# Attention stage: the input loads, the small transfers of the softmax sums and the shift row issued in another order on SyncE's queue

## The chip, the cores and the metric

The kernel runs on one core of a Trainium2 chip. Its time is the device time of one execution in microseconds, as a median of runs. Five engines work side by side, each through its own instruction stream: PE (TensorE, with its weight loads shown as PEld), DVE (VectorE), ACT (ScalarE), POOL (GpSimd) and SP (SyncE, which here only issues transfers). They wait for each other and for transfers by semaphores.

## The reference

```python
def reference(x, qkv_w, qkv_b, proj_w, proj_b, Wr, br, W1, b1, W2, b2):   # x: 4 x 2048 x 512, fp32
    xn = layernorm(x)
    # attention, 16 heads of 32
    qkv = einsum('bnc,dc->bnd', xn, qkv_w) + qkv_b
    q, k, v = split into heads
    attn = softmax(einsum('bhqd,bhkd->bhqk', q, k) * 32 ** -0.5)
    out = einsum('bhqk,bhkd->bhqd', attn, v)
    a = einsum('bnc,dc->bnd', out, proj_w) + proj_b
    # feed-forward: two of eight experts per batch, picked by the first token
    idx = top_k(xn[:, 0, :] @ Wr + br, 2)
    h = gelu(xn @ W1[idx] + b1[idx]);  f = sum(h @ W2[idx] + b2[idx]) / 2
    return x + a + f
```

## The kernel before

Three stages follow each other. `dense_stage` makes q, k, v and the feed-forward part and writes them to memory; `attention_stage` is the one that the diff touches; `output_stage` multiplies the attention's output by the projection and adds. Matrix products keep fp32 accuracy by splitting values into a high and a low part.

The attention stage works through 64 **groups** in order. A group is 512 query tokens of 4 heads against all 2048 keys. `it` numbers the 16 pairs of a batch and a set of four heads, `qc` the four query chunks of one `it`, so 16 times 4 groups. A group has 16 key tiles of 128 keys and 4 heads, so 64 **scores**: one matmul of 97x128 by 97x512 each (L1092, tile `st_ps`), counted by the semaphore `st_ready`. ACT takes the exponential of each (L932, `p_sb`, a ring of 7 key tiles).

PE's order inside a group is written out in `STEPS`, eight strings that are called blocks here, 0 to 7:

- "S" is a score. Three of the eight scores of a block stand ahead of its "V" and five behind it.
- "U" is a unit of the maximum search for a later group (L1021, `mx_ps`), which DVE reduces (L946, `unit_max`).
- "V" is the product of two earlier key tiles with the values (L1033, `o_ps`), 8 matmuls in the source.
- "T" in block 6 turns the row maxima round (L1026). ACT copies them to `shift` (L906), and SP writes that as one more row of `q_x` (L746, `load_shift`), which score 0 of the next group waits for.
- "Z" in blocks 7, 2 and 3 sums probabilities over keys by a matmul with ones (L1045, from `p_pair`).

POOL adds pairs of key tiles before those sums (`group`, `pair`, `join`): eight pair sums of 128x2048 (L855), called pair 0 to 7; four **joins**, transfers with addition of 1 MB from one buffer of `p_pair` into another (L859, issued by POOL on its own queue), called join 1 to 4; a last addition (L893); and, between pairs 5 and 6, `normalise` of the group before (L849, `o_inv` times `o_raw`). POOL waits for join 1 before it issues join 2, for join 2 before join 3, for join 3 before join 4, and for join 4 before pair 0 of the next group. PE's "Z" in block 2 of the next group waits for join 4.

The inverse of the sums goes by SP: `spread_sums` (L752) lays the sums out over partitions, DVE inverts them (L970), `store_inverse` (L756) writes them to memory, `spread_inverse` (L764, four transfers) reads them back into `o_inv`, spread over partitions, POOL normalises, and `store_group` (L770) writes the result.

SP also brings in the next inputs. `load(part, score)` waits until `st_ready` has counted `score` scores of the present group and then issues one 256 KB transfer: parts 0 to 3 are keys (L727; values, L732, where `qc` is 3), parts 4 to 6 are the three parts of one chunk of queries (L736). SP's queue is issued strictly in the order of the code, so whatever stands behind a waiting instruction waits too. ACT may write a key tile into `p_sb` only once POOL's pair sum of seven tiles before is done.

The functions that the diff touches:

Of the kernel before, what the change touches and what calls it, by code (L numbers as in the profile page):

```python
# [575 lines left out]
def attention_stage(nc, qh_d, ql_d, kh_d, kl_d, v_d, inv_d, o_d):  # L576
# [6 lines left out]
    QC = N // TOK  # L583
# [22 lines left out]
    with ctx:  # L606
# [38 lines left out]
        G = 2 * QC  # L645
# [26 lines left out]
        def reads(g, place, first, last):  # L672

            if place < 0:
                return reads(g - 1, place + PLACES, first, last)
            if g < 0 and not first:
                return -sum(step != "T" for _, _, step in FILLS[place + 1:])
            return sum(filled(step, j, n, first, last) for n in range(-2 if first else 0, g + 1)
                       for p, (j, _, step) in enumerate(FILLS) if n < g or p <= place)
# [4 lines left out]
        def read_count(L, g, place, first, last):  # L684
            n = reads(g, place, first, last)
            return n if first else (L * G + g + 1) * READS + (n + FIRST_READS - (G + g + 1) * READS)
# [35 lines left out]
        with nc.Block() as block:  # L722

            @block.sync
            def _(sp):
                def load_keys(it, u, h, part):
                    sp.dma_start(k_x[u][part * D:(part + 1) * D, h, :].bitcast(F32),  # L727
                                 (kh_d, kh_d, kl_d)[part][it, h * D:(h + 1) * D, :]).then_inc(k_ld[u], 16)

                def load_values(it, u, quarter):  # L730
                    kts = slice(quarter * KT // 4, (quarter + 1) * KT // 4)
                    sp.dma_start(v_sb[u][:, kts, :], v_d[it, :, kts, :]).then_inc(v_ld[u], 16)  # L732

                def load_query_part(it, qc, part):
                    src = (qh_d, ql_d, qh_d)[part]
                    sp.dma_start(q_x[qc][part * D:(part + 1) * D, :, :].bitcast(F32),  # L736
                                 src[it, :, qc * TOK:(qc + 1) * TOK].rearrange("(h d) n -> d h n", d=D)).then_inc(q_ld[qc], 16)

                def load_queries(it, qc):
                    for part in range(3):  # L740
                        load_query_part(it, qc, part)

                def load_shift(count, qc):

                    sp.wait_ge(shift_done, count)
                    sp.dma_start(q_x[qc][R:R + 1, :, :].bitcast(F32),  # L746
                                 shift[:, :].bitcast(F32)).then_inc(shift_ld, 16)

                def spread_sums(read):

                    sp.wait_ge(bank_read, read)
                    sp.dma_start(sum_t[:, :], sum_raw[0:P:D, :]).then_inc(sum_ld, 16)  # L752

                def store_inverse(count):
                    sp.wait_ge(inv_done, count)
                    sp.dma_start(inv_d.rearrange("h (r n) -> (h r) n", n=QR), inv_t[:, :]).then_inc(inv_st, 16)  # L756

                def spread_inverse(count):

                    sp.wait_ge(inv_st, count * 16)  # L760
                    if not (isinstance(count, int) and count == 1):
                        sp.wait_ge(o_st, (count - 1) * 16)
                    for h in range(4):
                        sp.dma_start(o_inv[h * D:(h + 1) * D, :], inv_d[h, :].partition_broadcast(D)).then_inc(inv_ld, 16)  # L764

                def store_group(turn0, it, qc, count):
                    dst = o_d[it, :, qc * TOK:(qc + 1) * TOK]
                    sp.lower_val(dst.offset * 4)
                    sp.wait_ge(o_done, count)
                    sp.dma_start(dst, o_inv[:, :]).then_inc(o_st, 16)  # L770


                load_queries(0, 0)
                for h in range(4):
                    for part, src in enumerate((kh_d, kh_d, kl_d)):
                        sp.dma_start(k_x[0][part * D:(part + 1) * D, h, :].bitcast(F32), src[0, h * D:(h + 1) * D, :]).then_inc(head_ld[h], 16)
                for qc in range(1, QC):
                    load_queries(0, qc)
                for quarter in range(4):
                    load_values(0, 0, quarter)  # L780
                load_shift(1, 0)

                def turn(L, first, last):
                    for g in range(G):
                        u, qc = g // QC, g % QC
                        it, more = L * 2 + u, not (last and u == 1)

                        def load(part, score):

                            if part < 4 and more:  # L790
                                sp.wait_ge(st_ready, L * G * SK + g * SK + score)
                                if qc < 3:
                                    load_keys(it + 1, 1 - u, (4 * qc + part) // 3, (4 * qc + part) % 3)
                                else:
                                    load_values(it + 1, 1 - u, part)
                            if part >= 4 and qc > 0 and more:
                                sp.wait_ge(st_ready, L * G * SK + g * SK + score)
                                load_query_part(it + 1, qc - 1, part - 4)
                            if part >= 4 and qc == 0 and not (first and u == 0):
                                sp.wait_ge(st_ready, L * G * SK + g * SK + score)  # L800
                                load_query_part(it, QC - 1, part - 4)

                        load(0, 20)
                        load(1, 20)
                        load(2, 24)
                        load(3, 24)
                        load(4, 28)
                        load(5, 28)
                        load(6, 30)
                        if not (first and g == 0):  # L810
                            spread_sums(read_count(L, g, PART_PLACE[LAST_PART], first, last))
                        if not (first and g == 0):
                            store_inverse(L * G + g)
                        if not (first and g == 0):
                            spread_inverse(L * G + g)
                        if not (last and g == G - 1):
                            load_shift(L * G + g + 2, (qc + 1) % QC)
                        if not (first and g == 0):
                            store_group(L, it - 1 if qc == 0 else it, (qc - 1) % QC, L * G + g)

                turn(0, True, False)
                for L in range(1, TURNS - 1):
                    turn(L, False, False)
                turn(TURNS - 1, False, True)
                spread_sums(ALL_READS + len(PARTS_AT) - PARTS_IN)
                store_inverse(NQ * QC)
                spread_inverse(NQ * QC)
                store_group(0, NQ - 1, QC - 1, NQ * QC)
                sp.wait_ge(o_st, NQ * QC * 16)
# [497 lines left out]
```

## Time and profile before

| | |
|---|---|
| median of 3 runs | 4755.97 us (4755.77 to 4758.41) |
| the profiled execution's own time | 4758.41 us |
| its span | 4756.6 us |
| busy share: PE, PEld, DVE, ACT, POOL | 98%, 62%, 66%, 50%, 68% |
| mean granted clock of TensorE | 0.985 |
| DMA moved, mean | 633.51 MB, 133 GB/s |
| POOL pair sums (L855) | 2471.6 us, 4875 ns each |
| PE scores (L1092) and units (L1021) | 1592.8 and 1573.2 us |

The span is what lies between the first and the last instruction of the profiled execution; it is 1.8 us shorter than that execution's own time. The attention stage fills about 3190 us of it. The share of POOL is an average over stages: it has little to do in the first and the last one.

### The profile page before, as it was taken

What the parts mean: (1) busy time and instruction counts of PE and PEld (TensorE: products, weight loads), DVE (VectorE), ACT (ScalarE), POOL (GpSimd) and SP (SyncE); (2) the same over time, 40 slices, a digit from 0 to 9 for tenths busy, and PEclk for the clock granted to TensorE, in tenths of its full rate; (3) what the DMA queues carried; (4) which work ended last, traced back from release to release, by engine and by line L of the source; (5) the groups of instructions that cost most, each with busy time, mean ns of one, the idle gap of its engine ahead of it and who ended that gap; (6) DMA issues with size and microseconds to landing.
All of it is one profiled execution on the core that took longest, in us unless ns stands there. A gap on an engine that the chain in (4) does not pass through costs nothing. (4 is left out here: it accounts for less than half of the span.)

```text
span 4756.6 us, 66549 instructions
## 1 busy us (share of the span) xinstructions
PE 4643.6 (98%) x24396; PEld 2966.5 (62%) x24396; DVE 3152.0 (66%) x5296; ACT 2397.4 (50%) x4653; POOL 3219.2 (68%) x1117
## 2 busy tenths in 40 slices
PE   8999999999989999999999999999999999999969
PEld 6887878878845555555555555555555555555447
DVE  4323232333178888888888888888888888888534
ACT  2112121121126666666666666666666666666621
POOL 1121212122249999999999999999999999999920
PEclk9999999999979999999999999999999999999989
DMA  5334342434245656656566665666656666565476
GB/s 168 111 115 135 101 147 81 135 118 131 71 111 126 139 131 137 135 130 138 131 136 134 134 138 130 138 133 135 135 131 138 132 136 134 130 138 123 92 230 236
DMA packets 261849, 633.51 MB, mean 133 GB/s; under 512 B 46741, under 2 KB 80533, under 8 KB 222617
## 3 DMA queue, kind: packets, MB, share of 16 engines
q0 software_dynamic: 36864, 268.45, 27.8%
q1 hardware_dynamic: 224664, 360.85, 26.7%
q8 instruction: 193, 3.16, 0.3%
q14 instruction: 128, 1.04, 0.1%
HBM read 224.96 MB, written 134.74 MB: 76 GB/s over the span
## 5 line engine op out<-in xcount | busy, mean ns | idle before, releaser
L946 DVE TENSOR_REDUCE unit_max<-mx_ps 128x1 f32<-128x512 f32 x4096 | 2501.8, 680 | 323.1 <-PE mx_ps L1021 320.9
L855 POOL TENSOR_TENSOR p_pair<-p_sb 128x2048 f32<-128x2048 f32 x512 | 2471.6, 4875 | 57.2 <-ACT p_sb L932 53.6
L932 ACT ACTIVATE p_sb<-st_ps 128x512 f32<-128x512 f32 x4096 | 2062.1, 628 | 863.0 <-PE st_ps L1092 862.8
L1092 PE MATMUL st_ps<-q_x,k_x 97*128 97x512 f32 x4096 | 1592.8, 410 | 3.4 <-ACT p_sb L932 2.5
L1021 PE MATMUL mx_ps<-k_x,q_x 96*128 96x512 f32 x4096 | 1573.2, 407 | 22.0 <-DMA k_x<-k_lo_d 20.0
L1092 PEld LDWEIGHTS st_ps<-q_x,k_x 97*128 97x128 f32 x4096 | 734.7, 189 | 537.3 <-issue 380.0
L1033 PE MATMUL o_ps<-p_sb,v_sb 128*32 128x512 f32 x8192 | 989.7, 601 | 0.0
L1021 PEld LDWEIGHTS mx_ps<-k_x,q_x 96*128 96x128 f32 x4096 | 782.8, 191 | 299.8 <-DVE unit_max L946 109.9
L285 POOL TENSOR_TENSOR h_lo<-h_f,h_hi 128x512 fp32r<-128x512 f32 x128 | 165.1, 1291 | 693.3 <-DVE h_hi L469 693.3
L1033 PEld LDWEIGHTS o_ps<-p_sb,v_sb 128*32 128x32 f32 x8192 | 214.1, 109 | 434.1 <-issue 280.8
L469 DVE CAST h_hi<-h_f 128x512 fp32r<-128x512 f32 x128 | 55.0, 431 | 543.5 <-ACT h_f L342 543.5
L342 ACT ACTIVATE h_f<-rot,b_sb 128x512 f32<-128x512 f32 x128 | 88.2, 689 | 647.9 <-PE rot L505 647.9
L859 POOL DMA_DIRECT2D p_pair<-p_pair x256 | 260.1, 1016 | 209.0 <-DMA p_pair<-p_pair 181.7
L893 POOL TENSOR_TENSOR p_pair<-p_pair 128x2048 f32<-128x2048 f32 x64 | 292.8, 4575 | 5.0
L326 ACT ACTIVATE qk_hi<-rot,qk_bias 128x512 fp32r<-128x512 f32 x128 | 88.2, 689 | 377.0 <-DMA q_lo_d<-qk_lo 164.6
L503 PE MATMUL rot<-xnT_hi,wq_hi 128*128 128x512 f32 x512 | 202.6, 396 | 17.5 <-DVE qk_lo L433 9.2
L1045 PE MATMUL mx_ps<-p_pair,ones 128*32 128x512 f32 x1536 | 201.9, 597 | 13.7 <-DMA p_pair<-p_pair 12.6
L503 PE MATMUL acc<-we_hi,h_hi 128*128 128x512 f32 x512 | 206.3, 403 | 7.4 <-POOL h_lo L285 5.7
L268 POOL TENSOR_TENSOR rstd<-var_eps,minus_half 128x4 f32<-128x4 f32 (+1 forms) x17 | 16.9, 992 | 284.3 <-DVE var_eps L372 284.3
L433 DVE SCALAR_TENSOR_TENSOR qk_lo<-rot,qk_bias,qk_hi 128x512 fp32r<-128x512 f32 x128 | 95.7, 748 | 161.1 <-ACT qk_hi L326 160.5
L505 PE MATMUL rot<-xnT_hi,wq_lo 128*128 128x512 f32 x512 | 201.3, 393 | 0.0
L504 PE MATMUL rot<-xnT_lo,wq_hi 128*128 128x512 f32 x512 | 201.3, 393 | 0.0
(94 smaller groups left out, 3812.5 us busy)
## 6 DMA issues: line engine op xcount, KB each, us to landing
p_pair<-p_pair POOLq DMA_DIRECT2D x256, 1024.0 KB, 7.5
q_x<-q_hi_d SPq DMA_DIRECT2D x128, 256.0 KB, 5.4
k_x<-k_hi_d SPq DMA_DIRECT2D x128, 256.0 KB, 3.9
xt<-x SPq DMA_DIRECT2D x64, 256.0 KB, 2.6
stage<-w SPq DMA_DIRECT2D x32, 512.0 KB, 5.0
q_hi_d<-qk_hi SPq DMA_DIRECT2D x64, 256.0 KB, 3.0
q_lo_d<-qk_lo SPq DMA_DIRECT2D x64, 256.0 KB, 3.8
k_hi_d<-qk_hi SPq DMA_DIRECT2D x64, 256.0 KB, 2.6
```

The source lines that it names most:

```text
L503: pe.matmul(out, lh, rh, start=start and k == 0, stop=False)
L504: pe.matmul(out, lh, rl, start=False, stop=False)
L505: op = pe.matmul(out, ll, rh, start=False, stop=stop and k == len(pairs) - 1)
L855: pool.tensor_tensor(p_pair[:, slot, :, :], p_sb[:, n % SLOTS, :, :], p_sb[:, (n + 1) % SLOTS, :, :], ALU.add).then_inc(pair_done, 1)
L859: pool.dma_start(p_pair[:, into, :, :], p_pair[:, slot, :, :], accum_op=ALU.add).then_inc(joined, 16)
L893: pool.tensor_tensor(p_pair[:, a, :, :], p_pair[:, a, :, :], p_pair[:, b, :, :], ALU.add).then_inc(pair_done, 1)
L932: act.activation(p_sb[:, (L * G * KT + n) % SLOTS, h, :], st_ps[bank(g, m)][:, :], ACT.Exp, scale=SCALE).then_inc(exp_done, 1)
L946: dve.reduce_max(unit_max[:, n // 4, n % 4:n % 4 + 1], mx_ps[UNIT_PLACE[n] % RING][:, :], AX.X).then_inc(bank_read, 1)
L1021: pe.matmul(mx_ps[UNIT_PLACE[n] % RING][:, :], q_x[qc][0:R, h, t * P:(t + 1) * P], k_x[u][0:R, h, kc * 512:(kc + 1) * 512], start=True, st ...
L1033: op = pe.matmul(o_ps[rows, :], v_sb[u][:, kt, rows], p_sb[:, (L * G * KT + n) % SLOTS, h, :], start=(kt == 0), stop=(kt == KT - 1))
L1045: op = pe.matmul(mx_ps[place % RING][h * D:(h + 1) * D, :], ones[:, :], p_pair[:, slot, h, :], start=True, stop=True)
L1092: pe.matmul(st_ps[bank(g, m)][:, :], k_x[u][:, h, kt * P:(kt + 1) * P], q_x[qc][:, h, :], start=True, stop=True).then_inc(st_ready, 1)
```

## The change

Inside each group, the code that SP runs is put in another order and its loads get other thresholds. The work itself, and the instructions of PE, DVE, ACT and POOL with their order, stay as they are.

```diff
-                        load(0, 20)
-                        load(1, 20)
-                        load(2, 24)
-                        load(3, 24)
-                        load(4, 28)
-                        load(5, 28)
-                        load(6, 30)
+                        load(0, 10)
+                        load(1, 10)
+                        load(2, 16)
+                        load(3, 16)
                         if not (first and g == 0):
                             spread_sums(read_count(L, g, PART_PLACE[LAST_PART], first, last))
+                        load(4, 33)
+                        load(5, 33)
                         if not (first and g == 0):
                             store_inverse(L * G + g)
+                        if not (last and g == G - 1):
+                            load_shift(L * G + g + 2, (qc + 1) % QC)
                         if not (first and g == 0):
                             spread_inverse(L * G + g)
-                        if not (last and g == G - 1):
-                            load_shift(L * G + g + 2, (qc + 1) % QC)
+                        load(6, 57)
                         if not (first and g == 0):
                             store_group(L, it - 1 if qc == 0 else it, (qc - 1) % QC, L * G + g)
```

SP's queue in a group with key loads (`qc` 1), before:

```order
L727 DMA k_x1<-k_hi_d 32x2048 [waits st_ready]
L727 DMA k_x1<-k_lo_d 32x2048 [waits st_ready]
L727 DMA k_x1<-k_hi_d 32x2048 [waits st_ready] x2
L736 DMA q_x0<-q_hi_d 32x4x512 [waits st_ready]
L736 DMA q_x0<-q_lo_d 32x4x512 [waits st_ready]
L736 DMA q_x0<-q_hi_d 32x4x512 [waits st_ready]
L752 DMA sum_t<-sum_raw 128x1x16 [waits bank_read]
L756 DMA inv_d<-inv_t 128x16 [waits inv_done]
L764 DMA o_inv<-inv_d 32x512 [waits o_st,inv_st]
L764 DMA o_inv<-inv_d 32x512 x3
L746 DMA q_x2<-shift 1x16x128 [waits shift_done]
L770 DMA o_d<-o_inv 128x512 [waits o_done]
```

The same group now:

```order
L727 DMA k_x1<-k_hi_d 32x2048 [waits st_ready]
L727 DMA k_x1<-k_lo_d 32x2048 [waits st_ready]
L727 DMA k_x1<-k_hi_d 32x2048 [waits st_ready] x2
L752 DMA sum_t<-sum_raw 128x1x16 [waits bank_read]
L736 DMA q_x0<-q_hi_d 32x4x512 [waits st_ready]
L736 DMA q_x0<-q_lo_d 32x4x512 [waits st_ready]
L756 DMA inv_d<-inv_t 128x16 [waits inv_done]
L746 DMA q_x2<-shift 1x16x128 [waits shift_done]
L764 DMA o_inv<-inv_d 32x512 [waits o_st,inv_st]
L764 DMA o_inv<-inv_d 32x512 x3
L736 DMA q_x0<-q_hi_d 32x4x512 [waits st_ready]
L770 DMA o_d<-o_inv 128x512 [waits o_done]
```

The sums' transfer has moved ahead of the queries, the shift row ahead of the four `o_inv` spreads, and the last part of the queries behind both. What has changed with the key loads is only the count that they wait for.

In the group with `qc` 3 the four first loads are values. SP's queue there before:

```order
L732 DMA v_sb1<-v_d 128x512 [waits st_ready] x4
L736 DMA q_x2<-q_hi_d 32x4x512 [waits st_ready]
L736 DMA q_x2<-q_lo_d 32x4x512 [waits st_ready]
L736 DMA q_x2<-q_hi_d 32x4x512 [waits st_ready]
L752 DMA sum_t<-sum_raw 128x1x16 [waits bank_read]
L756 DMA inv_d<-inv_t 128x16 [waits inv_done]
L764 DMA o_inv<-inv_d 32x512 [waits o_st,inv_st]
L764 DMA o_inv<-inv_d 32x512 x3
L746 DMA q_x0<-shift 1x16x128 [waits shift_done]
L770 DMA o_d<-o_inv 128x512 [waits o_done]
```

And now:

```order
L732 DMA v_sb1<-v_d 128x512 [waits st_ready] x4
L752 DMA sum_t<-sum_raw 128x1x16 [waits bank_read]
L736 DMA q_x2<-q_hi_d 32x4x512 [waits st_ready]
L736 DMA q_x2<-q_lo_d 32x4x512 [waits st_ready]
L756 DMA inv_d<-inv_t 128x16 [waits inv_done]
L746 DMA q_x0<-shift 1x16x128 [waits shift_done]
L764 DMA o_inv<-inv_d 32x512 [waits o_st,inv_st]
L764 DMA o_inv<-inv_d 32x512 x3
L736 DMA q_x2<-q_hi_d 32x4x512 [waits st_ready]
L770 DMA o_d<-o_inv 128x512 [waits o_done]
```

The same three moves are there, and the value loads too wait for lower counts.

## Rows read from the trace of the kernel before

**Rows 1.** Stretch; PE, PEld, DVE, ACT, POOL busy (instructions); granted clock, DMA share, GB/s.
```profile
1800.00:2200.00 400.00, 399.86 (x2288) 224.68 (x2280) 337.10 (x563) 267.56 (x536) 375.18 (x114) 1.00 0.62 136
```

**Rows 2.** Waits, 1300 to 4500 us: engine and line, releaser, total, times, longest.
```profile
POOL p_pair L859 <- DMA p_pair<-p_pair: 179.0, 67, 4.7
...
PE mx_ps L1045 <- DMA p_pair<-p_pair: 2.6, 7, 0.5
```

**Rows 3.** Timeline of POOL, one round: start, length, instruction, idle before.
```profile
2487.84 0.89 POOL L859 DMA_DIRECT2D p_pair<-p_pair  x1 [0.30 <-ACT p_sb L932]
...
2497.54 1.21 POOL L859 DMA_DIRECT2D p_pair<-p_pair  x1
...
2506.12 0.88 POOL L859 DMA_DIRECT2D p_pair<-p_pair  x1 [2.76 <-DMA p_pair<-p_pair]
...
2511.30 1.56 POOL L849 TENSOR_TENSOR o_inv<-o_raw,o_inv 128x512 f32<-128x512 f32 x1
2512.53 4.87 POOL L855 TENSOR_TENSOR p_pair<-p_sb 128x2048 f32<-128x2048 f32 x1
2517.07 1.18 POOL L859 DMA_DIRECT2D p_pair<-p_pair  x1
...
2527.48 9.15 POOL L855 TENSOR_TENSOR p_pair<-p_sb 128x2048 f32<-128x2048 f32 x2
2536.93 0.88 POOL L859 DMA_DIRECT2D p_pair<-p_pair  x1 [0.30 <-ACT p_sb L932]
```

**Rows 4.** Landing times of the joins issued at 2487.84, 2497.54, 2506.12, 2517.07.
```profile
DMA to landing us min/median/max: 7.6/7.6/7.6
...
DMA to landing us min/median/max: 8.1/8.1/8.1
...
DMA to landing us min/median/max: 7.0/7.0/7.0
...
DMA to landing us min/median/max: 7.2/7.2/7.2
```

**Rows 5.** Timeline of SP's transfers over the same groups.
```profile
2501.72 0.54 SPq L746 DMA_DIRECT2D q_x<-shift  x1
...
2526.68 2.67 SPq L732 DMA_DIRECT2D v_sb<-v_d  x4
...
2545.56 1.71 SPq L764 DMA_DIRECT2D o_inv<-inv_d  x4
2550.91 0.54 SPq L746 DMA_DIRECT2D q_x<-shift  x1
```

**Rows 6.** Timeline of PE: block 7's sums, scores 9, 15, 32, block 2's sums.
```profile
2506.85 1.04 PE L1045 MATMUL mx_ps<-p_pair,ones 128*32 128x512 f32 x8
...
2516.52 0.39 PE L1092 MATMUL st_ps<-q_x,k_x 97*128 97x512 f32 x1
...
2521.44 0.40 PE L1092 MATMUL st_ps<-q_x,k_x 97*128 97x512 f32 x1
...
2524.75 0.13 PEld L1045 LDWEIGHTS mx_ps<-p_pair,ones 128*32 128x32 f32 x4 [0.30 <-DVE unit_max L946]
...
2535.27 0.40 PE L1092 MATMUL st_ps<-q_x,k_x 97*128 97x512 f32 x1
```

**Rows 7.** Busy by stretch: first while queries load, second while keys load.
```profile
2534.00:2538.50 4.50, 4.50 (x29) 2.37 (x27) 4.50 (x8) 3.39 (x7) 4.20 (x3) 1.00 0.77 166
...
2577.00:2581.50 4.50, 4.50 (x32) 2.48 (x34) 4.50 (x8) 3.20 (x7) 4.50 (x2) 1.00 0.93 235
```

**Rows 8.** The shift transfers: count, duration, first and last start.
```profile
L746 SPq DMA_DIRECT2D q_x<-shift x64: 517/538/847, 1372.8 to 4474.4; - x64
```

**Rows 9.** The page's DMA issues, spreads: count, KB each, median us to landing.
```profile
o_inv<-inv_d SPq DMA_DIRECT2D x256, 64.0 KB, 2.1
```

**Rows 10.** Timelines at the attention stage's end: PE's last sums, POOL's last join.
```profile
4545.28 1.94 PE L1045 MATMUL mx_ps<-p_pair,ones 128*32 128x512 f32 x8 [10.01 <-DMA p_pair<-p_pair]
...
4537.93 1.18 POOL L859 DMA_DIRECT2D p_pair<-p_pair  x1
```

## What the change was predicted to do

> **What bounds the kernel now.** I read the busy shares by stretch first. In the attention stage PE is busy for 399.86 of 400 us, POOL for 375.18, at a full granted clock [rows 1]. So PE sets the pace and POOL runs close behind it. The waits say how close: PE waits for almost nothing, 2.6 us in all for joins that were late for its sums, seven times, 0.5 us at the longest [rows 2]. POOL waits for its own joins, 179.0 us in 67 waits [rows 2]. That is a loop on POOL that no other engine enters: while it waits for join 2 it does nothing else.
>
> Then the two clocks. The shift transfer leaves once a group, straight after block 6 of PE: 2501.72 and 2550.91, so a group takes 49.19 us on PE where nothing disturbs it [rows 5]. From 2501.72 to 4474.4, 40 groups, it is 49.32 on average [rows 5, 8], so some 0.13 us a group, about 8 us over 60 groups, is lost somewhere; the waits for joins show 2.6 of it. POOL's round from join 1 to join 1 is 2487.84 to 2536.93, 49.09 us [rows 3]. Inside it stands a wait of 2.76 us for join 2, which landed 8.1 us after its issue, while joins 3 and 4 took 7.0 and 7.2 [rows 3, 4]. With a join 2 of 7.1, POOL's round would be 48.1. So POOL is not slower than PE by its work; its late joins eat the one microsecond that it has in hand.
>
> The margin is thin at one place. Join 4 is issued at 2517.07 and landed by 2524.3; PE's sums in block 2 load their weights at 2524.75 [rows 3, 4, 6]. Half a microsecond more of lag on POOL and PE stalls. After PE's last product nothing covers POOL at all: PE's last sums wait 10.01 us for the join issued at 4537.93 [rows 10]. At the end of the stage each microsecond of POOL's lag is a microsecond of the program.
>
> **The change part by part.** No instruction is added or removed; 64 groups issue the same transfers at other moments. SP has little to do, so I cost the issue itself at nothing; what counts is which transfers share the DMA engines with which join, and who waits.
>
> *The shift row ahead of the four spreads.* SP waits for the shift at 2550.91 in any case; now the spreads stand behind it. They went out at 2545.56, 1 us before join 2 of that round (9.7 after 2536.93, by the spacing of the first two joins), so they shared the engines with its start [rows 3, 5]. Now they leave at 2550.91 + 0.54 = 2551.5, when join 2 is almost through. Join 2 should land in 7.0 to 7.2 where it took 8.1 [rows 4]; bounds 7.0 (all of the delay was theirs) and 8.3 (they only delay its end). I take 7.2: 0.9 us a group off POOL's round. The shift itself leaves as before. What hides the later spreads is the time until normalise. In the group before, the spreads would leave at 2502.3, end their issue at 2504.0 (1.71 us) and, with a landing of 2.1 as now, or 3 beside a join (my estimate), be there at 2506 to 2507; normalise starts at 2511.30 [rows 3, 5, 9]. The cover is 4.3 us or more, so nothing is lost.
>
> *Keys and values at counts 10 and 16.* The tenth score ends at 2516.9 and the sixteenth at 2521.8 [rows 6], where the loads of count 20 went out at 2526.68 [rows 5], when no join was under way (join 4 was down at 2524.3, the next came at 2536.93). Now the first two go out at the very moment of join 4 (2517.07) and the other two in the middle of it. Four key loads occupy the engines for 4.5 x 0.93 = 4.2 us [rows 7]. Join 4 therefore lands after 7.2 us at best and 7.2 + 4.2 = 11.4 at worst. At POOL's present lag that is 2524.3 to 2528.5, against 2524.75 for PE's sums and 2527.48 for pair 0: a stall of PE of up to 3.7 us and of POOL of up to 1.0 [rows 3, 6]. This is the part that could hurt. But a stall of PE moves PE back against POOL, so in the next group join 4 is earlier by as much: it is paid once, not 60 times, as long as POOL's own round is shorter than 49.19. Here the gain on join 2 decides.
>
> The Trainium skill, DMA: Bandwidth & Descriptors, section on queues, rings and completion order, says that each engine takes turns between the rings that have work, a packet at a time. By that rule the two loads issued 4.8 us behind the join take turns with its remainder, and it lands in 11.4; if instead it held its place against later ones, it would be 7.2 + 2.1 = 9.3. The rule speaks against the change, and no row here has a load that starts in the middle of a join; I keep 11.4 as the bound.
>
> *The queries.* Three loads took 4.5 x 0.77 = 3.5 us of the engines between 2534 and 2538.5 and so ran into join 1, issued at 2536.93 [rows 3, 7]. Now two go at count 33, 2535.7 [rows 6], 2.3 us of engine time, on top of join 1, and the third at count 57, beside join 3. A join 1 is in time if it lands within 8.8 us (two pair sums and the issue, 2487.84 to 2497.54, hide it) [rows 3]. Now it takes 7.0 + 2.3 = 9.3 at worst, 7.0 at best. I take 8.5, no cost, with 0.5 us a group as the bound. Join 3 has 10.95 us until join 4 (2506.12 to 2517.07) and needs at most 7.0 + 1.2 for the load and about 1 for the spreads; hidden.
>
> *The sums' transfer* goes out ahead of the queries, about a microsecond sooner; its consumer, the inverse, is not waited for. Nothing.
>
> **The sum.** POOL's round is 48.1 to 48.7 against 49.19 on PE, so POOL gains 0.5 to 1.0 us a group until something of PE's holds it. The nearest stops: pair 6 needs the sums of block 7, done at 2506.85 + 1.04 = 2507.89, and starts at 2512.53, 4.6 us of room; normalise has 4.3 [rows 3, 6]. So within some six groups POOL stands up to 4.3 us earlier against PE than now. There join 4 is issued at 2513, and even with 11.4 it lands at 2524.4, still ahead of 2524.75. Two gains follow. PE's stalls at block 2's sums go: 2.6 us by the waits, 8 at most by the averages; I take 3.5, near the row that names them. And at the end POOL's lag is smaller: 0 to 4.3 us; I take 3, since a late join throws POOL back now and then. In sum 6.5 us off the profiled execution's own 4758.41 us, which gives 4751.9; that execution was the slowest of three and 2.4 above their median, so by the median it is 4755.97 - 6.5 = 4749.5 us.
>
> **The rivals.**
>
> A, *the loads cost what the spreads give*. POOL's lag settles where it is now, because the loads on join 4 or the queries on join 1 take the microsecond back. For it: join 1 shares with two full loads, and PE's 399.86 of 400 leaves nothing to win elsewhere. Against it: both have cover and join 2 has none. Time 4756, give or take 2.
>
> B, *slower, by join 4*. Place: POOL's wait for join 4 ahead of pair 0, and PE's sums in block 2. Price: POOL's round becomes 49.09 (join 2 still at 8.1) + 0.5 (join 1) + 1.0 (join 4 at 11.4) = 50.6, 1.4 us over PE's 49.19, in 60 groups 84 us: 4840. It decides from the point where POOL's round is over 49.19, as then the stall of PE comes back in each group; just past that point it is 10 to 45 us, 4766 to 4800. Against it: the overlap shrinks as POOL gets ahead, and it needs join 2 to stay slow.
>
> C, *more than forecast*. All 8 us of lost time go, and the whole 4.3 of lag: 4755.97 - 12.3 = 4743.7. For it: late joins could be behind stalls that the waits don't name.
>
> That the loads don't go out sooner at all is excluded by SP's timeline: the store behind normalise is out by 2513, as normalise ends at 2512.86 [rows 3], four microseconds ahead of the tenth score.
>
> **How the numbers follow.** Forecast 0.50 (its own range 4746.5 to 4753), A 0.22, B 0.14, C 0.14. What can be told from no change is about 0.2%, 9.5 us. Faster by more than that is C and the edge of the forecast: 0.20. Slower is B with a little of A: 0.15. The rest, 0.65, is within. The range takes in the forecast, A and most of C: 4744 to 4760.
>
> **What would show it.** In the new profile the join issued third should follow the second by about 7.7 us instead of 8.6, and landing of join 2 should be near 7.1. Join 4 should land in 8 to 11 us. Join 4 should be issued 11 to 13 us behind the shift transfer instead of 15.35. PE's wait for joins should be gone in the steady stretch, and its wait at the stage's end about 7 us instead of 10.01. It is wrong if join 2 is no faster, if POOL waits for `o_inv`, or if PE waits for joins in most groups.

## The result, and the profile after

The changed kernel takes 4825.27 us (median of 5, 4807.03 to 4840.70) against 4758.41 us (median of 5, 4755.77 to 4764.59) for the kernel before. The ratio on record is 1.0119, 95% interval 1.0094 to 1.0145, so it is slower by 1.2%. That is less than the quotient of these two medians (1.014); the 15 executions of the changed kernel that are on record have a median of 4814.71 us. The prediction was 4749.5 us, range 4744 to 4760, and is wrong. The profiled execution took 4816.15 us, span 4814.3.

The loss lies in the attention stage: from the first shift transfer to the last it was 3101.6 us [rows 8] and is now 3159.1, 57.5 us more, which is nearly the difference of the spans, 57.7. The shift transfers of the changed kernel (count, duration, first and last start):

```profile
L746 SPq DMA_DIRECT2D q_x<-shift x64: 518/548/613, 1374.2 to 4533.3; - x64
```

Busy time in the stretch of [rows 1] (PE, PEld, DVE, ACT, POOL, clock, DMA share, GB/s) in the changed kernel:

```profile
1800.00:2200.00 400.00, 393.51 (x2239) 220.08 (x2237) 329.91 (x549) 261.89 (x525) 364.82 (x112) 1.00 0.60 132
```

PE, which hardly rested before, now does. Its waits, and POOL's, from 1300 to 4500 us (total, times, longest), beside [rows 2]:

```profile
POOL p_pair L859 <- DMA p_pair<-p_pair: 144.8, 65, 3.8
POOL o_inv L849 <- DMA o_inv<-inv_d: 71.1, 24, 4.4
...
PE mx_ps L1045 <- DMA p_pair<-p_pair: 43.7, 32, 3.8
...
POOL p_pair L855 <- DMA p_pair<-p_pair: 10.6, 12, 2.4
```

PE waits 43.7 us for joins where it waited 2.6, in 32 groups, and POOL waits 71.1 us for the spreads of `o_inv`, where it waited once, 2.6 us. POOL's wait for its joins fell from 179.0 to 144.8. One round of POOL in the changed kernel, beside [rows 3]:

```profile
2406.38 0.88 POOL L859 DMA_DIRECT2D p_pair<-p_pair  x1 [0.30 <-ACT p_sb L932]
...
2416.07 1.18 POOL L859 DMA_DIRECT2D p_pair<-p_pair  x1
...
2424.09 0.88 POOL L859 DMA_DIRECT2D p_pair<-p_pair  x1 [2.22 <-DMA p_pair<-p_pair]
...
2433.61 1.28 POOL L849 TENSOR_TENSOR o_inv<-o_raw,o_inv 128x512 f32<-128x512 f32 x1 [4.07 <-DMA o_inv<-inv_d]
...
2439.40 0.87 POOL L859 DMA_DIRECT2D p_pair<-p_pair  x1
...
2449.49 9.16 POOL L855 TENSOR_TENSOR p_pair<-p_sb 128x2048 f32<-128x2048 f32 x2
2458.94 0.88 POOL L859 DMA_DIRECT2D p_pair<-p_pair  x1 [0.30 <-POOL p_pair L855]
```

The round is 52.56 us. Joins 2 and 3 are 8.02 apart, where they were 8.58: join 2 is quicker, as forecast. Between joins 3 and 4 there are 15.31 us instead of 10.95, with 4.07 of waiting for `o_inv`. SP's transfers over the same time, beside [rows 5]:

```profile
2422.72 0.55 SPq L746 DMA_DIRECT2D q_x<-shift  x1
2423.37 2.45 SPq L764 DMA_DIRECT2D o_inv<-inv_d  x4
2425.86 1.29 SPq L736 DMA_DIRECT2D q_x<-q_hi_d  x1
...
2438.12 0.32 SPq L727 DMA_DIRECT2D k_x<-k_hi_d  x1
2438.48 0.42 SPq L727 DMA_DIRECT2D k_x<-k_lo_d  x1
2443.00 1.59 SPq L727 DMA_DIRECT2D k_x<-k_hi_d  x2
```

The spreads leave from 2423.37 on, and join 3 is issued among them, at 2424.09, 0.7 us behind the first. How long these four took, and then the four of the group before, of which the first had left 1.3 us ahead of join 3 (issue to landing):

```profile
DMA to landing us min/median/max: 2.0/4.4/8.2
...
DMA to landing us min/median/max: 2.0/2.0/2.2
```

In these two groups a spread took 2.0 us where it went out well ahead of the join, and up to 8.2 us beside it. The key loads leave at 2438.12 and 2438.48, here ahead of join 4 (2439.40), which then landed after 8.3 us where it took 7.2 [rows 4]. Over the groups the first key load leaves between 1.3 us ahead of join 4 and 3.0 us behind it, 1.0 us behind on average. PE in block 2 of that group, and in the group that begins at about 2030 us:

```profile
2447.88 1.06 PE L1045 MATMUL mx_ps<-p_pair,ones 128*32 128x512 f32 x8 [1.37 <-DMA p_pair<-p_pair]
...
2048.57 1.06 PE L1045 MATMUL mx_ps<-p_pair,ones 128*32 128x512 f32 x8 [2.91 <-DMA p_pair<-p_pair]
2049.57 0.98 PE L1092 MATMUL st_ps<-q_x,k_x 97*128 97x512 f32 x2
2050.35 0.63 PE L1021 MATMUL mx_ps<-k_x,q_x 96*128 96x512 f32 x1
2050.78 0.63 PE L1092 MATMUL st_ps<-q_x,k_x 97*128 97x512 f32 x1
...
2053.32 0.39 PE L1021 MATMUL mx_ps<-k_x,q_x 96*128 96x512 f32 x1
```

After the longer stall a matmul takes 0.63 us instead of 0.39 for the next three microseconds. The stretches before and after that point (PE busy is the number behind the comma, the granted clock the third from the end):

```profile
2043.00:2048.40 5.40, 2.66 (x20) 0.72 (x18) 2.65 (x5) 1.33 (x3) 4.34 (x1) 1.00 0.83 193
2048.60:2053.00 4.40, 4.40 (x17) 2.81 (x18) 2.51 (x4) 1.96 (x4) 4.40 (x1) 0.64 0.00 0
2056.00:2060.00 4.00, 4.00 (x30) 2.17 (x23) 2.16 (x5) 1.71 (x4) 3.70 (x3) 1.00 0.16 33
```

So part of a long stall's price comes behind it, as a stretch at the lower level of the clock. By the clock records, PE spends 23.9 us of 1500 to 4500 there, against 3.4 us before (those in one piece, at 4483 us).

At the end of the stage nothing was gained:

```profile
4602.80 1.93 PE L1045 MATMUL mx_ps<-p_pair,ones 128*32 128x512 f32 x8 [10.17 <-DMA p_pair<-p_pair]
```

It was 10.01 [rows 10].

### The profile page after: what moved, and what is told of

It is laid out like the page before. It is cut to its first block and busy times, and to the rows that moved or that the text cites. A ratio compares the mean times of both kernels' runs of the same rounds, so it can differ in the third digit from the quotient of the medians.

```text
span 4814.3 us, 66549 instructions
## 1 busy us (share of the span) xinstructions
PE 4657.6 (97%) x24396; PEld 2969.0 (62%) x24396; DVE 3154.2 (66%) x5296; ACT 2398.8 (50%) x4653; POOL 3220.0 (67%) x1117
## 5 line engine op out<-in xcount | busy, mean ns | idle before, releaser
L859 POOL DMA_DIRECT2D p_pair<-p_pair x256 | 246.1, 961 | 179.4 <-DMA p_pair<-p_pair 149.7
L963 DVE TENSOR_TENSOR sum_raw<-mx_ps,sum_raw 128x512 f32<-128x512 f32 x128 | 88.5, 692 | 216.3 <-PE mx_ps L1045 216.3
```

The source lines that it names most:

```text
L859: pool.dma_start(p_pair[:, into, :, :], p_pair[:, slot, :, :], accum_op=ALU.add).then_inc(joined, 16)
```

## The experiments

The change has three parts: **F**, keys and values at counts 10 and 16; **S**, the shift ahead of the spreads; **Q**, the sums' transfer first, two queries at 33 and the third at 57. After the result I held two theories: S (the spreads run into join 3, the 71.1 us) and F (the key loads run into join 4). The first runs do each part alone, or undo one. All ratios are to the kernel before on the same chip (medians 4761.31, 4759.91 and 4760.15 us on the three chips used), with a 95% interval. The diffs here are shortened: several calls stand on one line, and `...` stands for arguments or lines left out.

**F alone.**

```diff
-load(0, 20) load(1, 20) load(2, 24) load(3, 24)
+load(0, 10) load(1, 10) load(2, 16) load(3, 16)
```

> The kernel before with one part of the change: the keys and values loaded at counts 10, 10, 16, 16. Theory S: the spreads leave before the shift as before, POOL never waits for o_inv; join 4 lands in 8 to 9 us, PE stalls a little while POOL's lag adapts; 4750 to 4768 us. Rival F: PE waits for join 4 in some 30 groups, 40 us or more, 4795 us or more.

Measured: 4820.97 us, 1.0130 (1.0114 to 1.0145). F was right, and S, which I thought the likelier, wrong: this part alone costs as much as the whole change. The waits:

```profile
PE mx_ps L1045 <- DMA p_pair<-p_pair: 40.3, 25, 3.5
POOL o_inv L849 <- DMA o_inv<-inv_d: 18.2, 10, 2.5
```

And the clock behind one of its stalls of 3.1 us:

```profile
2049.00:2055.00 6.00, 6.00 (x20) 4.13 (x13) 3.88 (x6) 2.97 (x6) 6.00 (x2) 0.54 0.00 0
```

**S alone.**

```diff
-spread_inverse(...)
 load_shift(...)
+spread_inverse(...)
```

> The kernel before with one part of the change: the shift row issued ahead of the four o_inv spreads. Theory S (the spreads, issued behind the shift, run into join 3; they landed 8 to 10 us after their issue there, and POOL waited 3 to 5 us for o_inv in 24 groups): POOL waits for o_inv, 15 to 70 us in all, join 4 is late by as much, PE waits for it; 4770 to 4810 us. Rival F (the early key loads on join 4 are what stalls PE): no loads lie on join 4 here, so 4750 to 4762 us.

Measured: 4757.06 us, 0.9992 (0.9983 to 1.0001), no difference that can be told. POOL waits 7.1 us for `o_inv` before 4500 us, PE 0.3 us for joins. Theory S, that the move by itself is the cause, falls.

**Q alone.**

```diff
-load(4, 28) load(5, 28) load(6, 30)  spread_sums(...)
+spread_sums(...)  load(4, 33) load(5, 33)
 store_inverse(...) spread_inverse(...) load_shift(...)
+load(6, 57)
```

> The kernel before with one part of the change: the sums' transfer ahead of the queries, two query loads at count 33 and the third at 57, the spreads ahead of the shift as before. Theory S and rival F both expect little: 4750 to 4765 us. A third view, that the query loads on joins 1 and 3 set the time, expects 4780 us or more.

Measured: 4767.58 us, 1.0017 (1.0008 to 1.0026), slightly over what was expected. In the profiles PE's wait at the stage's end is 13.31 us, where it was 10.01; in the steady stretch it waits 3.9 us for joins.

**S undone in the changed kernel** (the spreads ahead of the shift again).

> The changed kernel with one part undone: the four o_inv spreads ahead of the shift row again. Theory S: POOL's waits for o_inv (71 us in the changed kernel) are gone and with them nearly all of PE's waits for join 4; 4748 to 4768 us. Rival F: the loads still lie on join 4, 4800 us or more.

Measured: 4801.41 us, 1.0092 (1.0077 to 1.0107), as F said. The interval overlaps that of the changed kernel, so no share of S is shown by it.

**F undone in the changed kernel** (counts 20, 20, 24, 24).

> The changed kernel with one part undone: keys and values at counts 20, 20, 24, 24 again. Theory F: join 4 lands in 7.0 to 7.5 us, PE's stalls are gone but for 10 us at the stage's end; 4753 to 4768 us. Theory S (the spreads behind the shift are a cause of their own once the third query load stands behind them): 4785 us or more.

Measured: 4759.42 us, 1.0001 (0.9992 to 1.0010). With S and Q in and F out, the loss is gone.

**Q undone in the changed kernel** (queries at 28, 28, 30, ahead of the sums' transfer).

> The changed kernel with one part undone: the queries at counts 28, 28 and 30 ahead of the sums' transfer again, the loads of counts 10 and 16 and the shift ahead of the spreads kept. Theory F: join 4 still lands in 8.5 us or more, 4800 to 4825 us. If the third query load behind the spreads is what makes the spreads collide with join 3 in the changed kernel (71 us of waits for o_inv there, 17 with the shift moved alone), those waits fall under 40 us here and the time is 10 to 20 us under the changed kernel's.

Measured: 4796.90 us, 1.0072 (1.0059 to 1.0086). A little under what F expected. The waits for `o_inv` fell from 71.1 to 34.4 us, so part Q as a whole adds to them; which of its moves does, this run doesn't separate.

The four kernels that have F don't add up: F alone 1.0130, with S 1.0072, with Q 1.0092, with both 1.0119. Each of S and Q takes something off the loss of F alone (the intervals don't overlap), and the two together don't. Nor does POOL's wait for `o_inv` tell the order: it is 18.2, 34.4, 10.1 and 71.1 us in these four. No run shows why.

**The keys earlier still.** This tells "early" from "on top of join 4".

```diff
-load(0, 20) load(1, 20) load(2, 24) load(3, 24)
+load(0, 1)  load(1, 1)  load(2, 1)  load(3, 1)
```

> The kernel before, with the four key or value loads at count 1 instead of 20 to 24, so earlier still than in the change, but done before join 4 starts to move data. Theory F (it is the overlap with join 4 that costs, as join 4 has half a microsecond of margin): join 4 lands in 7.0 to 7.6 us, PE waits for it no more than before; 4752 to 4765 us. Rival E (loads early in a group are bad as such, for instance because the keys' buffers or SP's queue are late for something else): 4790 us or more, as with counts 10 and 16.

Measured: 4764.31 us, 1.0011 (1.0002 to 1.0020). Early as such is no cause: the loss is 0.1% where counts 10 and 16 cost 1.3%. Join 4 was expected in 7.0 to 7.6 us and takes 7.83 (to its last packet, as below), so even loads 3.8 us ahead of it aren't quite free, and PE's wait at the stage's end is 13.31 us against 10.01. PE's wait for joins before the stage's end:

```profile
PE mx_ps L1045 <- DMA p_pair<-p_pair: 4.8, 12, 1.1
```

**The first pair alone**, and **two loads meant for the second half of join 4**, both on the kernel before.

```diff
-load(0, 20) load(1, 20) load(2, 24) load(3, 24)
+load(0, 10) load(1, 10) load(2, 24) load(3, 24)     # the first
+load(0, 16) load(1, 16) load(2, 24) load(3, 24)     # the second
```

> The kernel before with the first two key or value loads at count 10, the other two at 24 as before. Theory F, by what join 4 did beside all four loads (its first data held up some 1.2 us by the first two, its last ones by the other two): join 4 lands in about 8 us, half of the loss; 4770 to 4795 us. If only the second pair matters: 4755 to 4765 us.

> The kernel before with the first two key or value loads at count 16 and the other two at 24 as before, so that two loads run into the second half of join 4 and none into its start. Theory F: join 4 lands in about 8 us; 4765 to 4790 us. If a join that has started is not held up by later loads: join 4 lands in 7.2 us and the time is 4755 to 4762 us.

Measured: 4800.32 us, 1.0074 (1.0060 to 1.0088), and 4767.21 us, 1.0013 (1.0004 to 1.0022). The first came out somewhat above what was expected, the second in it. By the packets in the traces, issue to last packet, mean of groups 4 to 59, join 4 takes 7.25 us in the kernel before, 8.72 with two loads issued beside it, 7.37 with two issued 5.5 us behind it, 8.82 with all four. So the two loads around the join's issue do nearly all of its delay. They don't do all of the loss, though: 0.74% and 0.13% are less than 1.30%, so the mean of join 4 alone doesn't give the price. And the second run doesn't show what its expectation asks: the first packet of its loads comes 7.0 us behind the join's issue, when the join is all but done, so it hardly had an overlap. The waits, first and second kernel:

```profile
PE mx_ps L1045 <- DMA p_pair<-p_pair: 29.3, 30, 2.5
```

```profile
PE mx_ps L1045 <- DMA p_pair<-p_pair: 7.0, 13, 0.9
```

**Normalise later.** In the changed kernel, on POOL.

```diff
 pair(at, 5, c)
-if at > 0: normalise(at)
 ...
 pair(at, 6, a)
 ...
 join(d, c)
+if at > 0: normalise(at)
 pair(at, 7, b)
```

> The changed kernel with normalise moved on POOL from between pairs 5 and 6 to behind join 4, so that join 4 is issued 1.2 us sooner and does not wait for o_inv. Theory F with S as its second part: the share of the spreads goes (the waits for o_inv no longer delay join 4), and join 4 has 1.7 us of margin instead of 0.5, so most of PE's stalls go: 4755 to 4775 us. If the loads' overlap alone is stronger than that margin: 4785 to 4805 us.

Measured: 4812.96 us, 1.0115 (1.0099 to 1.0130), which neither side expected. PE waits for no join at all in the steady stretch, but a new wait stands in its place: ACT copies the next group's product only when normalise is done, and PE then waits for ACT in every group.

```profile
ACT o_raw L912 <- POOL o_inv L849: 148.1, 61, 2.7
...
PE st_ps L1092 <- ACT p_sb L932: 38.1, 62, 0.9
```

It doesn't show what the lack of margin cost, and it moves the overlap too: the key loads now come 5.4 us behind join 4 instead of 1.0, and the join takes 6.85 us. The next run keeps the overlap.

**The sums later.** In the changed kernel, with all its loads and POOL's order, PE's two sums stand one block later.

```diff
-PARTS = [(2, 0, False, 7), (4, 0, True, 10), (0, NA, False, 11)]
+PARTS = [(2, 0, False, 7), (4, 0, True, 11), (0, NA, False, 12)]
     # and the "Z" of block 2 of STEPS goes to block 4
```

> The changed kernel with PE's two sums of blocks 2 and 3 one block later, in blocks 3 and 4, so that the sum behind join 4 has some 6 us more margin; all loads and joins as in the changed kernel. Theory F (join 4 lands 1.5 us later on average, up to 5, against 0.5 us of margin, and PE stalls): PE's waits for join 4 are gone before the stage's end, no stretch at the lower clock follows; 4750 to 4765 us. Rival P (POOL's own round has grown over 49.2 us by the loads and would hold PE through its pair sums anyway): 4785 us or more, with ACT or PE waiting for pair sums.

Measured: 4765.41 us, 1.0014 (1.0005 to 1.0023), just above the upper end of what F expected. Join 4 is even slower (9.10 us, against 8.79 in the changed kernel), but PE waits for it only at the stage's end, and there is no stretch at the lower clock between 1500 and 4500 us.

```profile
PE mx_ps L1045 <- DMA p_pair<-p_pair: 10.3, 1, 10.3
```

POOL's round came back to 49.43 us with the same loads, from 50.29. So nearly all of the harm of the late join comes by PE's stall, and rival P falls. (POOL's wait for `o_inv` fell as well, to 21.0 us; that S undone still costs 0.92% says that this isn't what saved the time.) The 0.14% that are left over aren't placed. One wait is new, of DVE for the sums' transfer, which now leaves a block later, and no row shows that PE pays for it:

```profile
DVE inv_t L970 <- DMA sum_t<-sum_raw: 29.3, 21, 2.2
```

**Loads in the gaps.** Keys at count 1, queries at 20, the shift ahead of the spreads.

Against the changed kernel:

```diff
-load(0, 10) load(1, 10) load(2, 16) load(3, 16)
+load(0, 1) load(1, 1) load(2, 1) load(3, 1) load(4, 20) load(5, 20) load(6, 20)
 spread_sums(...)
-load(4, 33) load(5, 33)
 store_inverse(...) load_shift(...) spread_inverse(...)
-load(6, 57)
 store_group(...)
```

> A kernel that puts the loads into the gaps between the joins: keys and values at count 1 (ahead of join 4), the queries at count 20 (between joins 4 and 1), the shift ahead of the spreads as in the change. By theory F the joins run alone: join 1 lands in under 7.8 us, join 2 in 7.1, join 4 in 7.8; POOL's round is free to be under 49.2 and PE waits for no join before the end; 4748 to 4758 us. If the spreads behind the shift throw POOL back as often as in the changed kernel: 4760 us or more.

Measured: 4758.54 us, 0.9993 (0.9984 to 1.0002), just above what was expected and not to be told from the kernel before. Joins 1 and 2 are quick (6.98 and 7.28 us, where they took 8.29 and 7.59), join 4 is slower than before (7.94 against 7.25). PE waits 1.5 us for joins, so there was little left to win, and POOL waits 26.9 us for `o_inv` instead of getting ahead. No version was shown to beat the kernel before.

**What the long stalls have in common.** No run was made for this; it is read from the traces. The profile's DMA queues q8 and q14 carry instructions, in packets of 16 and 8 KB, with 193 and 127 or 128 packets whatever the version (here the kernel before; packets, MB, share of the engines):

```profile
q8 instruction: 193, 3.16, 0.3%
q14 instruction: 128, 1.04, 0.1%
```

Where one of these packets comes within 7 us of join 4's issue, the join is slower, also in the kernel before: 7.92 us in 15 groups against 7.01 in the other 41. With F alone it is 10.08 in 12 groups against 8.47 in 44, in the changed kernel 10.04 in 9 against 8.55 in 47. In twelve profiles (all but those of the moved normalise and the moved sums) PE waited for a join 174 times between 1510 and 4500 us. All 42 waits of 1.5 us and more, and so all 29 that were followed by the lower clock, have such a packet between the join's issue and the wait's end. With F alone long waits (2.4 us and more) stand at 1595, 2049, 2500, 2953, 3406, 3859 and 4313 us, nine groups apart. So the loads make join 4 late by 1.5 us in nearly all groups, and the worst stalls are those groups in which an instruction packet adds about as much again.

## Why the prediction was wrong

*What bounds the kernel, and where it is thin:* right. PE sets the pace, and join 4 has half a microsecond at block 2. Most of the loss (51 of 57.5 us, below) came in there.

*Join 2 becomes quick:* right. 7.02 us on average against 7.59, 7.96 us between joins 2 and 3 against 8.58.

*The shift ahead of the spreads, "nothing is lost":* the cover was mis-sized. I took 3 us for a spread beside a join; it is up to 8.2. The 4.3 us of cover don't hold that, hence 24 waits of normalise. The trace of the kernel before had it already: the last of the four spreads took over 5 us in 35 of 64 groups, up to 8.6, and POOL waited for it once. The median of 2.1 over all 256 hid that, and so did the one round that I read. Alone, the move cost nothing that can be measured; POOL waited for `o_inv` only 3 times.

*Keys and values at counts 10 and 16, "it is paid once, not 60 times":* this is the step that failed. I had the place, the margin and the worst landing (11.4). Join 4 went from 7.25 to 8.79 us on average, and PE's stall came back in 32 groups: 41 us more of waits, and 20.5 us more at the lower clock behind them. The argument that a stall puts POOL ahead for good needed a POOL round under 49.19 us. I had worked out 48.1 to 48.7; POOL's joins are 50.29 apart on average (10.06 + 7.96 + 12.35 + 19.92 between the joins, against 9.85 + 8.58 + 10.94 + 19.92). This average alone doesn't say who sets the pace: two engines that wait for each other go round in the same time, and PE's shift transfers are 50.14 apart too (3159.1 over 63). But with the same loads and no stall (the sums later) POOL's joins are 49.43 apart: the loss hangs on the stalls. I had also judged the margin by one group with a join 4 of 7.2 us, where over groups 4 to 59 it takes 6.9 to 8.9 in the kernel before and up to 11.3 in the changed one; with loads and an instruction packet beside it, a lag that fits the other groups stalls PE again.

Why the lead that a stall gives POOL is lost again, no run separates. One way would be that SP's transfers follow PE's counts. When PE is pushed back against POOL, they slide onto joins that they used to miss: with F alone join 1 takes 9.15 us instead of 8.29, though the query loads have the same counts. By itself that isn't enough, since with S alone join 1 takes 9.11 and nothing is lost.

*The clock:* not in the sum at all. The arithmetic of the profiled pair: PE's waits for joins 43.7 - 2.6 = 41 us; 23.9 - 3.4 = 20.5 us more at half the clock, which lose about half of that (17 matmuls in 4.4 us, where a stretch at full clock has 30 in 4.0), 10 us; 51 of 57.5 us. The other 6 I can't place.

*The queries:* join 1 took 8.60 us against 8.29, within my bounds. Q alone costs 0.17%, where I had taken none.

*The stage's end:* wrong; the wait there is 10.17 us against 10.01, where I had 7. What holds it isn't shown: it is 9.84 with S alone, 12.01 with F alone and 13.31 with Q alone.

*The rivals.* B had the right sign, place and size (4766 to 4840 covers 4825), but I tied it to a slow join 2. That condition was false: join 2 is quick, and the joins stand further apart behind joins 3 and 1 (12.35 against 10.94, 10.06 against 9.85). I gave it 0.14.

*The rule of the Trainium skill* (DMA: Bandwidth & Descriptors, section on queues, rings and completion order), that an engine takes turns between rings: the traces agree only in part. Taking turns, a load that comes 2 to 3 us behind the join should get through beside it. In the 64 such groups of the five kernels with the first pair at count 10 (instruction packets aside, the run with later sums left out), its first packet comes 7.2 us behind the join's issue, when the join is nearly done; a load issued just ahead of the join has it after 1 us. So what was queued first mostly went first, and a join held a spread for 6 us. Still those joins take 8.19 us against 7.01, so they are not untouched. The worst groups did reach 10 to 12 us, with an instruction packet in play.

## What to carry to other kernels

Look for the transfer with the least margin before the bounding engine, and keep other transfers away from its issue: here from a microsecond ahead of it to three behind. Loads a few microseconds further off, in either direction, cost 0.1% instead of 1.3%. Judge a margin by its worst groups and not by one, and look at instruction packets too; don't take the median of small transfers for their time beside a big one. Don't count a repeated stall as paid once because the engines shift against each other. Check a margin by widening it, as the run with the later sums did.

## What the runs showed of the hardware

- A short stall of TensorE can be charged twice. Of the 174 waits of PE for a join (twelve profiles, 1510 to 4500 us) none of the 132 under 1.5 us was followed by the lower level of the clock (1.2 instead of 2.4 GHz); of the 20 from 1.5 to 2.5 us 9 were, and of the 22 longer ones 20. The granted clock was 0.54 over the 6 us behind a wait of 3.1 us. F alone has 41.0 us at the lower level between 1500 and 4500 us.
- A transfer of 64 KB took 2.0 us to land, and up to 8.2 us when a 1 MB transfer with addition was issued from POOL's queue beside it.
- Loads of 256 KB (a pair around its issue, in four of five kernels a second pair some 5 us later) made such a 1 MB transfer slower by up to 1.9 us, by when the first was issued: 7.01 us without loads, 8.40 with the first load up to 0.5 us ahead of it, 8.93 up to 0.5 us behind, 8.19 at 2 to 3 us behind, 7.03 with a single pair 5 to 7 us behind (to its last packet, groups without an instruction packet).
- Instruction packets of 8 or 16 KB share the DMA engines with the program's transfers: one of them within 7 us of the issue goes with a 1 MB transfer of 7.92 us where the others take 7.01 (kernel before, 56 groups).
